# Preparing the first local tiles inside attention, normalising earlier in the feed-forward, and dropping dummies from the first local step

## The reference

```
h = concat(einsum('bhid,oi,od->bho', x, weighted_sum, weight), txt)
# linear attention, 16 heads of 64
q, k = elu(LN(h) @ Wq) + 1, elu(LN(h) @ Wk) + 1;  g = sigmoid(LN(h) @ Wg + bg)
kv = sum_n k v^T;  z = 1 / max(q . sum_n k, 1e-6)
h = h + ((q * SCALE) @ kv * z * g) @ Wo
# two layers on y = LN(h), each:
#   local stage: shift half the channels by a token, q k v = y @ wqkv,
#     l2norm of q and k, scales, rotary turn, softmax over a window of
#     128 tokens and the 128 before it, 8 heads of 64, y = y + o @ wo
#   feed-forward: shift, LayerNorm, a, g = y @ w1 + b1, y = y + (a * gelu(g)) @ w2 + b2
h = h + y
```

## Time and profile before

| what | value |
|---|---|
| median of three runs | 1840.4 us |
| the profiled execution | 1838.76 us |
| its span (first to last instruction) | 1837.0 us |
| mean granted TensorE clock | 0.996 of full |
| TensorE busy | 1781.5 us (97%) |
| VectorE busy | 1398.3 us (76%) |
| ScalarE busy | 1003.6 us (55%) |
| GpSimd busy | 528.1 us (29%) |

### The profile page before, as it was taken

How to read it: one execution, slowest core, us unless ns; L and a number is a source line. 1 busy time by engine, 2 the same in 40 slices (tenths; PEclk the granted TensorE clock), 3 DMA queues, 4 the chain that set the end, 5 groups by cost and what they waited for, 6 DMA issues and landing times. The chain is left out here.

```text
span 1837.0 us, 52994 instructions
## 1 busy us (share of the span) xinstructions
PE 1781.5 (97%) x19826; PEld 1561.2 (85%) x19826; DVE 1398.3 (76%) x4325; ACT 1003.6 (55%) x2481; POOL 528.1 (29%) x382
## 2 busy tenths in 40 slices
PE   8999999999999899999999899999999999989998
PEld 7879889889888688888888788888888888878887
DVE  5877877877767678888888677767888888867774
ACT  4443443443433288888887444337777777743332
POOL 0000000000000266666666000025666666601111
PEclk9999999999999999999999999999999999999999
DMA  9200000000020111111111200002111111110010
GB/s 323 87 1 2 1 1 2 1 2 2 1 72 2 55 25 29 26 29 27 27 29 33 98 12 12 0 1 69 29 26 29 28 28 28 33 31 9 10 65 33
DMA packets 64830, 60.44 MB, mean 33 GB/s; under 512 B 16415, under 2 KB 59211, under 8 KB 64718
## 3 DMA queue, kind: packets, MB, share of 16 engines
q1 hardware_dynamic: 64718, 58.88, 10.8%
HBM read 33.95 MB, written 8.39 MB: 23 GB/s over the span
## 5 line engine op out<-in xcount | busy, mean ns | idle before, releaser
L1222 ACT ACTIVATE l_probs<-l_probs,l_negmax 128x192 f32<-128x192 f32 x512 | 225.8, 442 | 90.7 <-DVE l_negmax L1333 90.7
L1046 POOL TENSOR_TENSOR l_t<-l_t,l_rnorm 128x512 f32<-128x512 f32 x128 | 136.4, 1085 | 246.4 <-DVE l_rnorm L1000 246.4
L1169 POOL TENSOR_TENSOR l_probs<-l_probs,l_rowinv 128x768 f32<-128x768 f32 x128 | 185.1, 1466 | 16.5 <-DVE l_rowinv L1357 16.5
L117 PE MATMUL ps<-local_w_hi,l_xT 128*128 128x512 f32 x384 | 157.7, 411 | 3.4 <-DVE l_xT L1039 2.1
L1177 POOL TENSOR_TENSOR l_t<-l_t,l_t 128x1024 f32<-128x1024 f32 x63 | 149.1, 2367 | 40.5 <-DVE l_t L1014 28.9
L1159 POOL MEMSET l_xT<- 128x520 f32 x1 | 0.5, 531 | 553.4 <-POOLq L463 553.4
L118 PE MATMUL ps<-local_w_lo,l_xT 128*128 128x512 f32 x384 | 151.2, 394 | 0.0
L119 PE MATMUL ps<-local_w_hi,l_xT 128*128 128x512 f32 x384 | 150.9, 393 | 0.0
L117 PE MATMUL ps<-m_hnT_hi,ffn_w_hi 128*128 128x512 f32 (+1 forms) x352 | 141.6, 402 | 0.0
L499 ACT ACTIVATE attn_exp<-ps 128x512 f32<-128x512 f32 x128 | 76.4, 599 | 117.0 <-PE ps L119 117.0
L119 PE MATMUL ps<-m_hnT_hi,ffn_w_lo 128*128 128x512 f32 (+1 forms) x352 | 139.2, 396 | 0.0
(11 more groups left out here) (262 smaller groups left out, 5773.8 us busy)
## 6 DMA issues: line engine op xcount, KB each, us to landing
l_edge<-l_v SPq DMA_DIRECT2D x252, 64.0 KB, 2.0
tok_x<-x SPq DMA_DIRECT2D x16, 512.0 KB, 8.2
shifted<-x SPq DMA_DIRECT2D x64, 64.0 KB, 1.5
m_shifted<-shifted SPq DMA_DIRECT2D x16, 256.0 KB, 2.9
out<-x SPq DMA_DIRECT2D x8, 512.0 KB, 3.8
ffn_w_raw<-ffn_w SPq DMA_DIRECT2D x6, 640.0 KB
local_w_raw<-ffn_wqkv SPq DMA_DIRECT2D x4, 768.0 KB, 5.7
tok_base<-attn_base SPq DMA_DIRECT2D x4, 512.0 KB, 8.9
```

Source lines behind the costliest of these rows:

```text
L117: nc.tensor.matmul(out, wh, mh, start=start, stop=False, skip_group_check=True)
L1046: return nc.gpsimd.tensor_tensor(v, v, rn[:, a * LH:(a + 1) * LH].unsqueeze(2).to_broadcast([P, LH, DH]), ALU.mult)
L1169: nc.gpsimd.tensor_tensor(v, v, rinv[:, heads].unsqueeze(2).to_broadcast([P, LH // 2, REACH]), ALU.mult).then_inc(s.normal.sem, 1)
L1222: last = nc.scalar.activation(v, v, ACT.Exp, bias=nb[:, h:h + 1], scale=-1.0, accum_out=rsum[:, h:h + 1])
```

## The change

1. The last stage of attention's last batch also prepares tiles 0 and 1 of layer 0's local stage: ScalarE normalises and splits them (`x_copy`, `x_hi`), TensorE transposes them (`x_t`) and projects both (`qk`), VectorE does low parts, turns both (`turn`) and forms the inverse norm of tile 0, GpSimd adds and scales, and TensorE transposes the turned tile 0 (`turned_t`). `outputs` of group 2 moves ahead of the Wo product. Both layers' local stages now start at step 1.
2. For that, the places in memory change: the gate's weights come first and the keys' second, and x's tiles of the local stage lie first in their region.
3. The late statistics go behind steps 2 and 3 of the local stage.
4. In the first local step, of both layers, all dummies are dropped, and the sum of squares comes first on VectorE.
5. In the feed-forward, `normalise` goes from behind chunk 2 to between its product and its low part.

The core of the diff:

```diff
@@ attention_phase, GpSimd
+            pool.wait_ge(*s.attn_kv_mm.after(B))
+            nc.gpsimd.memset(lxt[:, 1].bitcast(F32), 0.0).then_inc(ls.set.sem, 1)
+            pool.wait_ge(*ls.turned.after(1))
+            nc.gpsimd.tensor_tensor(t1[:], t1[:], t2[:], ALU.add).then_inc(ls.summed.sem, 1)
+            pool.wait_ge(*ls.summed.after(1))
+            pool.wait_ge(*ls.rnorm.after(1))
+            for a in range(2):
+                scaled_window(nc, t1, rn, a).then_inc(ls.rotated.sem, 1)
@@ ScalarE, last stage and tail
+                    if last and u == STAGES - 1:
+                        act.wait_ge(*ls.set.after(1))
+                        x_hi(0)
                     tanh_(b, 2 * u + 1)
...
+                    if last and u == 2:
+                        x_copy(0)
+                        x_copy(1)
...
             batches(act, batch)
+            act.wait_ge(*ls.x_done.after(1))
+            x_hi(1)
+            squares(0)
...
+            squares(1)
@@ VectorE, last stage and tail
-                    gated(b, u, 0, 1)
+                    gated(b, u, 0)
+                    if last and u == STAGES - 1:
+                        x_lo(0)
+                    gated(b, u, 1)
+                    if last and u == STAGES - 1:
+                        x_lo(1)
+                        gated(b, u, 2)
+                        turn(0)
                     residual(b, last, u, 1)
...
-            gated(B - 1, STAGES - 1, 2)
+            nc.vector.tensor_reduce(ss[:], sq[:].rearrange("p a (h d) -> p (a h) d", d=DH), AX.X,
+                                    ALU.add).then_inc(ls.sq_summed.sem, 1)
             last_lo(0)
+            dve.wait_ge(*ls.sq_summed.after(1))
+            for k in range(10):
+                chain(rnorm_step(nc, k, rn, ltmp, ss))
+            rnorm_step(nc, 10, rn, ltmp, ss).then_inc(ls.rnorm.sem, 1)
             last_lo(1)
             h_stats(B - 1, True, STAGES - 1)
-            for which in range(2):
-                last_residual(which)
+            last_residual(0)
+            turn(1)
+            last_residual(1)
@@ TensorE, last stage and tail
+                    if last and u == STAGES - 1:
+                        x_t(0)
+                        x_t(1)
                     outputs(b, u, 0)
...
+                    if last and u == STAGES - 1:
+                        outputs(b, u, 2)
+                        pe.wait_ge(*ls.w_lo.after(len(K.quarters) - 1))
+                        qk(0)
                     out_products(b, last, u, 1)
-                    outputs(b, u, 2)
+                    if not (last and u == STAGES - 1):
+                        outputs(b, u, 2)
...
+            qk(1)
             for which, (hi, lo) in enumerate(((oth, otl), (oth2, otl2))):
+                if which:
+                    turned_t()
@@ local_phase, ScalarE, start
+            x_copy(2, 0)
+            if layer == 0:
+                nc.scalar.activation(kt[:, :, 0], ps[:, TQ].rearrange("p (m t) -> p m t", t=P),
+                                     ACT.Copy).then_inc(s.qk_done.sem, 1)
+                normalise(X[:, 0:1], 0).then_inc(s.x_kept.sem, 1)
@@ local_phase, VectorE
+            def between(n):
+                if layer == 0 and n == 2:
+                    K.tile_stats(late, T).variance(nc, chain)
+                if layer == 0 and n == 3:
+                    K.tile_stats(late, T).deviation(nc, chain)
...
@@ local_phase, TensorE, first step
                 if second:
                     project(1 - r, 2, V).then_inc(s.v_full.sem, 1)
-                    keep_warm(nc, K, OT, 6)
...
-                if second:
-                    keep_warm(nc, K, OT, 18)
@@ mlp_phase, VectorE
+                    if c == 2:
+                        between = lambda: normalise(g + 1, 1 - r)
...
-                    if c == 2:
-                        normalise(g + 1, 1 - r)
```

140 lines of the change are left out of this document (82 added, 58 removed).

## The result

The changed kernel takes 1818.6 us (median of 4 runs, 1815.0 to 1820.5) against 1840.5 before (1835.8 to 1843.8). The ratio is 0.988, with a 95% interval of 0.985 to 0.991: 1.2% faster, where 1819 had been predicted. The profiled execution took 1819.65 us, its span is 1817.9; the sum of the prediction gave 1817.2 for such an execution.

What follows compares the result with a forecast made beforehand. TensorE was taken as the bound everywhere, busy 97% of the span. Terms -11.1 - 2.05 - 4.1 - 2.6 - 1.7 = -21.6 us took 1838.76 to 1817.2; the median 1.6 above gave 1819, range 1811 to 1829.

Steps and rivals of the forecast that it cites:

- Part 1: End of attention: the added preparation work makes the last products end 5.8 us later; bounds 4.1 and 10.5.
- Part 2, local start: Layer 0's local stage: second scores 15.5 us after the start in place of 33.4, minus 17.9; bounds minus 17.0 and 19.0.
- late statistics: Layer 0's local stage: 19 small VectorE steps moved behind steps 2 and 3 cost plus 1.0 us; bounds 0 and 3.7.
- rival B: End of attention: VectorE and GpSimd block one another, 2.4 + 2.2 us, giving 1823.6; chance 0.05.
- Part 3: Layer 1's first local step: without dummies and with the reduction first, minus 2.05 us; bounds minus 1 and minus 2.4.
- Part 4: Feed-forward: earlier normalisation saves waits of 4.1 us in layer 0 and 2.6 in layer 1, and a clock fall of 1.7.
- rival C: First two local steps: clock falls at new pauses, three of 1.7 us, none saved in layer 1; 1826, chance 0.08.
- Part 5: Memory places, queue order, GpSimd's clearing, ScalarE's copies of x and SyncE's changed wait: these cost nothing.
- A: End of attention: VectorE becomes the bound, having gained 9.5 us of work; 1826, chance 0.11.
- D: Feed-forward gives its gain back because the later low part of chunk 2 delays its products; 1827, chance 0.06.
- E: Local stage: its earlier start is eaten by another wait, only the feed-forward's 8.4 us is kept; 1832, chance 0.05.
- F: Local stages' loops: another phase makes the clock fall repeatedly, slower than before, for example 1867; chance 0.03.

Runs made afterwards that it cites:

- run 11: The changed kernel itself, measured once more on the same chip and in the same rounds as the last group of runs; 1816.3 us.
- runs 1, 2: In the changed kernel, 19 steps replace the late statistics at the same places: first one-input element-wise steps, 1818.6 us; then 17 of them reductions, 1813.9 us.
- run 3: In the changed kernel, ScalarE's wait for the late statistics was moved from ahead of the loop to inside it, before the copy of x; 1816.8 us.
- run 6: In the changed kernel, the 6 and the 18 dummies in layer 1's first local step were put back; 1821.3 us.
- run 5: In the changed kernel, the feed-forward normalises behind chunk 2 again, as before the change; 1828.0 us.

## Why the prediction was right, and where it was not

The total and the range were right, 1819 for 1818.6, and so was the mechanism of every part but one, the late statistics. Between the two profiles the sum came out 2.5 us short (-19.1 for -21.6). The late statistics were 4.5 us dearer than their term, 1.6 of it a fall of the clock, and 0.9 came up to attention's tail; attention's tail and the local start were 0.7 us better each, and the second feed-forward 1.45. The first gave more than its term as well, but a fall in the drain took 1.2 us of it. So the errors went both ways, and that the median was met to 0.4 us is luck: the same kernel measured 1816.3 us in run 11. No run takes parts 1 and 2 back; what they bring is read from the stretches of the two traces.

- **Part 1, attention's tail: right.** +5.1 for +5.8. The products end at 624.4, the stage starts at 626.1. The wait for the first low part is 1.16 us for the 1.5 foreseen, that for the residual 0.16, and the 0.3 foreseen for the gating did not come.
- **Part 2, local start: right.** The second scores come 14.8 us after the start for 15.5. The first masked score came at 629.88, 3.8 us in instead of 4.4, because the mask's transfer let VectorE go after 2.7 us and not 3.25, and the low part overlapped the next step.
- **Part 2, late statistics: wrong in size.** The sentence "The first eight steps (1.65) fit nearly, the other eleven (2.25) push the reciprocal by 0.8 ... I take plus 1.0 in all; bounds 0 and 3.7" took 0.2 us for every step, beside the scalings too. Measured +5.5, and +3.9 where the clock doesn't fall (13.48 + 14.03 against 23.59), both beyond the upper bound, and steps 3 and 4 took over 13 us, which the prediction had named as the sign of being wrong. Four of the 19 steps are held for 0.75 us each beside GpSimd's scalings (runs 1, 2), and the wait in front of the loop adds 0.7 to TensorE's pause (run 3). The bound was no bound: it counted only the steps' own time. The mechanism was written down as rival B, down to "the statistics meet the scalings", but it got 0.05 because the rule of the Trainium skill that run 2 names was tried on the low parts and rotations, which go free, and not on the statistics, to which it applies. Its other half did not come: the addition ends at 614.26 and the norm's first step starts at 614.39. The price of a tiny step could have been read from the trace of before. There a `TENSOR_SCALAR` on two elements per partition (L1039) falls 61 times of 66 beside GpSimd's addition, ends each time with it and takes 0.77 to 1.1 us; alone it takes 0.16 to 0.22. VectorE, then GpSimd:

```profile
867.20 0.78 DVE L1039 TENSOR_SCALAR l_xT<-l_xT 128x2 fp32r<-128x2 f32 x1
```

```profile
865.57 2.37 POOL L1177 TENSOR_TENSOR l_t<-l_t,l_t 128x1024 f32<-128x1024 f32 x1 [0.56 <-DVE l_t L1014]
```

- **Part 3, dummies: right.** -2.15 for -2.05, and +2.16 when they are put back (run 6).
- **Part 4, feed-forward: right in mechanism, too small.** The waits went to 0.3 us, as said for layer 0 (layer 1's rest of 0.6 didn't show). The waits were taken at the length that the rows show; each has 0.16 us more behind it, 1.1 in seven. By run 5 the two layers together give 9.2 us in the trace, for 6.7.
- **Part 4, clock, and rival C: neither shown nor refuted.** The term of -1.7 took one fall as the fixed price of the wait of 1.95 us. After the change the clock stood at 1.00 there, as forecast, but three falls came elsewhere in the profiled execution, one of them behind a new pause and none in the first two local steps that rival C named; in run 11 none came. That a fall behind a pause of some 2 us is chance is shown for the drains and for the pause in step 4. For the wait of 1.95 us it is not: only one profile has it, and in run 5 the wait came back as one of 1.70 us, without a fall. Without its falls the first profile after would be some 4 us shorter, and that of before some 1.7.
- **Part 5: right**, as far as shown: the loops kept their length within 0.2 us.
- A, D, E and F did not come. VectorE's second rotation lies beside TensorE's products, the products of chunk 2 wait for nobody, and both loops run at 11.9 us a step.

The 0.9 us up to attention's tail hold a fall worth 1.5 us and 0.6 us the other way. The 0.6 lie in the start of the program: the pause near 125 us ends at 125.96 before and 125.33 after, and over the thirteen profiles it ends anywhere from 124.3 to 126.0, whatever the kernel. Not settled: why one execution has falls at three pauses and the next at none.

## What to carry to other kernels

Before small VectorE steps are moved into a gap, look at what GpSimd does in that gap: here element-wise steps on SBUF were held to the end of its instruction even at two elements per partition (0.78 us for 0.16), while reductions and steps that read PSUM were not, and behind single scores all 19 steps cost 1.1 us together. Ask also who waits for the moved step in front of a loop. A TensorE wait that the profile showed as 0.2 us cost 0.36, so that many short ones are worth more than their sum. Take no single clock fall as the price of one pause: look at several executions, and where a pause of some 2 us has room for dummies that nobody waits for, fill it.

## What the runs showed of the hardware

- VectorE's `TENSOR_SCALAR`, `TENSOR_TENSOR` and `SCALAR_TENSOR_TENSOR` from SBUF to SBUF in fp32 on as little as 128x8 took 0.90 to 0.97 us instead of 0.17 beside a GpSimd instruction of 1.04 us and ended with it; `TENSOR_REDUCE` on the same tile took 0.17, 0.2 from start to start. Low parts that read PSUM (0.64 to 0.69) kept their time.
- The clock fell from 2.4 to 1.2 GHz behind pauses of 1.9 to 2.2 us in some executions and not in others, at the same code: 3 of 13 at 1.9 us (the pause near 125 us), 3 of 6 at 2.1 (step 4) and 12 of 20 at 2.2 (the drains). A fall cost 1.6 us in step 4 (15.65 against 14.03) and 1.2 to 1.3 in the drains.
- The same kernel spans 1813.3 and 1817.9 us in two profiles, of which three falls explain 4.3 of the 4.6 us.
